# Adjacency build of a graph network kernel: narrow one-hots made four at a time on VectorE, a smaller share on GpSimd, and registers loaded in eights

## What is computed

```
x = layernorm(x + GCN(x))      # three rounds of  relu(layernorm(A_norm (h W) + b)),  A with self loops
x = layernorm(x + SUM(x))      # A (x W^T + b)
x = layernorm(x + GIN(x))      # two-layer MLP with batch norm of (1 + eps) x + A x
x = layernorm(x + RGCN(x))     # two rounds, per relation: mean over the edges of one type, summed
```

## Time and profile before

| | |
|---|---|
| median of 3 runs | 3174.41 us (3173.7 to 3174.66) |
| the profiled execution | 3173.94 us, span of its record 3172.1 us |
| build, from the first product to the last copy out of a bank | 67.3 to about 469.7 us |
| first and last transpose issued | 81.8 and 461.0 us (24 of them, 23 octaves between) |
| VectorE busy in those 379.2 us | 346.9 us |
| granted TensorE clock in them | 0.86 of full |

### The profile page before, as it was taken

The page is one execution under the profiler, slowest core; times in us unless marked ns, Lnnn a source line. Parts: engine busy times, 40 slices in busy tenths (PEclk is TensorE's granted clock), DMA queues, the critical chain, the costliest instruction groups (busy, mean ns, idle before and its releaser), DMA issues.

```text
span 3172.1 us, 51345 instructions
## 1 busy us (share of the span) xinstructions
PE 1767.6 (56%) x10220; PEld 947.7 (30%) x10220; DVE 1839.9 (58%) x6822; ACT 409.3 (13%) x868; POOL 1859.6 (59%) x2045
## 2 busy tenths in 40 slices
PE   4766669998954444444444446984444444444447
PEld 2222225444432222222222225762222222222227
DVE  6989986896334544444444445664444444444445
ACT  2444441111130000000000002530000000000003
POOL 2777760000027777777777773127777777777773
PEclk8888888999975555555555557995555555555558
DMA  2443440017022222222222221122222222222221
GB/s 62 102 104 96 93 114 7 1 38 222 1 60 57 53 54 53 54 53 54 53 54 53 53 54 44 79 76 53 54 53 54 53 54 53 54 53 54 53 54 30
DMA packets 174998, 191.76 MB, mean 60 GB/s; under 512 B 110508, under 2 KB 140989, under 8 KB 174722
## 3 DMA queue, kind: packets, MB, share of 16 engines
q0 software_dynamic: 50048, 102.60, 12.4%
q10 hardware_dynamic: 84924, 40.88, 5.5%
q1 hardware_dynamic: 39750, 45.01, 4.3%
HBM read 130.57 MB, written 38.14 MB: 53 GB/s over the span
## 4 chain that ended last, share of the span: by engine, by line
POOL 40%; PE 19%; issue 14%; DVE 13%; DMA 7%; SPq 4%; ACTq 2%; ACT 1%; DVEq 0%; POOLq 0%
POOL adj L775 40%; DMA adj<-table,adj 6%; DVE hi_hot L1240 6%; PE banks L552 5%; PE banks L537 4%; SPq L421 3%; PE banks L671 3%; DVE lo_hot L1248 2%; PE banks L683 2%; PE banks L723 1%; DMA adj_copy<-adj 1%; SPq L374 1%; DVE deg_in L1408 1%; PE banks L656 1%; PE banks L509 1%
## 5 line engine op out<-in xcount | busy, mean ns | idle before, releaser
L775 POOL DMA_INDIRECT adj<-table,adj x1564 | 1478.8, 946 | 511.2 <-issue 455.0
L627 PE MATMUL banks<-adj 128*128 x3908 | 807.0, 285 | 1174.3 <-DVE adj L1535 772.7
L1550 DVE TENSOR_TENSOR adj<-adj,banks 128x129 f32 x1954 | 566.0, 290 | 1000.0 <-PE banks L627 920.6
L627 PEld LDWEIGHTS banks<-adj 128*128 128x128 f16 x3908 | 406.5, 104 | 1579.9 <-issue 1534.3
L1535 DVE TENSOR_SCALAR adj<-adj 128x128 f16<-128x128 f16 x1954 | 550.8, 282 | 1.5
L755 POOL TENSOR_SCALAR lo_hot<-minus_iota,zT 128x128 f16<-128x128 f16 x392 | 312.3, 813 | 143.8 <-PE banks L509 92.0
L509 PE MATMUL banks<-hi_hot,lo_hot 128*128 128x400 f16 x977 | 273.8, 392 | 141.3 <-DVE hi_hot L1240 64.6
L1240 DVE TENSOR_SCALAR hi_hot<-iota,zT 128x400 f16<-128x400 f16 x977 | 271.5, 339 | 32.9 <-PE banks L509 32.2
L762 POOL MEMSET adj<- 128x32 f16 x1 | 0.1, 127 | 421.6 <-PE banks L552 421.6
L552 PE MATMUL banks<-adj,split 128*128 128x512 f16 (+1 forms) x1078 | 216.8, 359 | 0.0
L509 PEld LDWEIGHTS banks<-hi_hot,lo_hot 128*128 128x128 f16 x977 | 103.4, 106 | 312.0 <-issue 259.3
(11 more groups left out here) (242 smaller groups left out, 1280.1 us busy)
## 6 DMA issues: line engine op xcount, KB each, us to landing
adj<-table,adj POOLq DMA_INDIRECT x1564, 2.5
adj_copy<-adj ACTq DMA_DIRECT2D x25, 800.0 KB, 3.9
adj<-adj_copy SPq DMA_DIRECT2D x6, 2176.0 KB, 16.4
table<-adj SPq DMA_DIRECT2D x25, 512.0 KB, 2.6
adj<-adj_copy SPq DMA_DIRECT2D x1, 3072.0 KB, 10.4
adj<-adj_copy SPq DMA_DIRECT2D x3, 1024.0 KB, 15.7
table<-split SPq DMA_DIRECT2D x6, 256.0 KB, 2.3
out_dram<-xres SPq DMA_DIRECT2D x6, 256.0 KB
```

The costliest lines, as they stand in the source:

```text
L627: m = e.matmul(bank[j % NSUM][:, 0:b - a], hot[:, j % NHOT, :], edge[:, a:b], start=(q == 0), stop=(q == 1), skip_group_check=True)
L775: e.indirect_dma_start(gath[:, (t + 1) % NG, 0:2 * D], None, table, bass.IndirectOffsetOnAxis(ap=index[:, which, t:t + 1].bitcast(U32), ax ...
L1550: e.tensor_tensor(a, a, bank[j % NSUM][:, 0:D + 1], ALU.add).then_inc(accumulated, 1)
```

## The change

Four things are changed in the build.

1. VectorE makes the narrow one-hots of a group with one `tensor_tensor` of 128 x 4 elements instead of four `tensor_scalar` of 128. The slot then holds the four steps interleaved, column by column, so TensorE takes its stationary operand with a step of four elements for those groups (`by_column`). GpSimd's groups keep the old layout (`by_step`). The comparison is now with a positive row (`iota`, `iota4`), and the plan writes the edge's number twice, as fp32 (`nlo`) and as fp16 (`lo`).
2. GpSimd makes one group of three, 82 instead of 98 of the 245. VectorE makes 163.
3. There are ten slots for wide one-hots instead of eight, and they are made eight steps ahead instead of six.
4. SyncE and ScalarE load their registers eight at a time instead of 32: 31 loads instead of 8, and 25 instead of 7. TensorE's loads stay.

```
-POOL_SHARE = (2, 5)
+POOL_SHARE = (1, 3)
+GATES, ENDS = 8, 8
...
+        lo = zT[:, 3 * JA - JA // 2 - 1:3 * JA].bitcast(F16)
...
-        NLO, NHI, NWIN = 8, 8, 8
-        AHEAD_LO, AHEAD_HI = 5, 6
+        NLO, NHI, NWIN = 8, 10, 8
+        AHEAD_LO, AHEAD_HI = 5, 8
...
-        minus_iota = sb("minus_iota", [P, P], F16, own)
-        lo_hot = sb("lo_hot", [P, NLO, LG, P], F16, own)
+        iota4 = sb("iota4", [P, P, LG], F16, own)
+        lo_hot = sb("lo_hot", [P, NLO, P * LG], F16, own)
+        by_step = lo_hot.rearrange("p s (k n) -> p s k n", n=P)
+        by_column = lo_hot.rearrange("p s (n k) -> p s n k", k=LG)
...
             for g in range(NGATE):
-                if g % REGS == 0:
-                    n = min(REGS, NGATE - g)
+                if g % GATES == 0:
+                    n = min(GATES, NGATE - g)
                     e.load(gate_regs[0:n], gate_row[:, g:g + n])
...
-                e.matmul(banks[:, bass.ds(c, 1), 0:NC].rearrange("p o n -> p (o n)"), lo_hot[:, g % NLO, j % LG, :],
+                low = by_step[:, g % NLO, j % LG, :] if by_pool(g) else by_column[:, g % NLO, :, j % LG]
+                e.matmul(banks[:, bass.ds(c, 1), 0:NC].rearrange("p o n -> p (o n)"), low,
                          hi_hot[:, j % NHI, :], start=False, stop=True, skip_group_check=True).then_inc(crossed, 1)
...
-                    e.tensor_scalar(lo_hot[:, g % NLO, k, :], minus_iota[:, :], nlo[:, j:j + 1], None,
+                    e.tensor_scalar(by_step[:, g % NLO, k, :], iota[:, 0:P], nlo[:, j:j + 1], None,
                                     ALU.is_equal).then_inc(low_pool, 1)
...
             for w in range(NWA):
-                k = w % REGS
+                k = w % ENDS
                 if k == 0:
-                    n = min(REGS, NWA - w)
+                    n = min(ENDS, NWA - w)
                     e.load(end_regs[0:n], end_row[:, w:w + n])
...
-                e.tensor_scalar(nlo[:, a0:a0 + n], sets[0][:, 0:n], -1.0, None, ALU.mult).then_inc(own_dve, 1)
+                e.tensor_copy(lo[:, a0:a0 + n], sets[0][:, 0:n]).then_inc(own_dve, 1)
+                own.up()
+                e.tensor_copy(nlo[:, a0:a0 + n], sets[0][:, 0:n]).then_inc(own_dve, 1)
...
-                    for j in steps_of(g):
-                        e.tensor_scalar(lo_hot[:, g % NLO, j % LG, :], minus_iota[:, :], nlo[:, j:j + 1], None,
-                                        ALU.is_equal).then_inc(low_dve, 1)
+                    k, n = g * LG, len(steps_of(g))
+                    e.tensor_tensor(by_column[:, g % NLO, :, 0:n], iota4[:, :, 0:n],
+                                    lo[:, k:k + n].unsqueeze(1).broadcast_to([P, P, n]), ALU.is_equal).then_inc(low_dve, 1)
```

More of the change, by code:

```diff
@@ L145, in gnn_stack @@
         gate_row = zT[64:65, 2 * JA:2 * JA + NGATE].bitcast(I32)
-        assert 3 * JA + NWA <= NP and NWORD <= JA and NGATE <= JA
+        assert 3 * JA + NWA <= NP and NWORD <= JA // 3 and NGATE <= JA // 3
         tab_i = carve([P, 3, TB, P], I32)
@@ L294, in gnn_stack @@
         for g in range(NG_LO):
-            made[by_pool(g)] += len(steps_of(g))
+            made[by_pool(g)] += len(steps_of(g)) if by_pool(g) else 1
             low_at[g] = made[by_pool(g)]
@@ L367, in _ @@
             e.dma_start(scr_t, rows_i[:, 1, :]).then_inc(plan_out, 16)
-            gate_regs = [e.alloc_register(f"gate{i}") for i in range(REGS)]
+            gate_regs = [e.alloc_register(f"gate{i}") for i in range(GATES)]
             least = e.alloc_register("least_free")
@@ L371, in _ @@
             for g in range(NGATE):
-                if g % REGS == 0:
-                    n = min(REGS, NGATE - g)
+                if g % GATES == 0:
+                    n = min(GATES, NGATE - g)
                     e.load(gate_regs[0:n], gate_row[:, g:g + n])
-                e.reg_alu(least, gate_regs[g % REGS], 1, ALU.max)
+                e.reg_alu(least, gate_regs[g % GATES], 1, ALU.max)
                 e.wait_ge(window_free, least)
@@ L745, in _ @@
                    allow_small_or_imprecise_dtypes=True).then_inc(iotas_set, 1)
-            e.iota(minus_iota[:, :], pattern=[[-1, P]], base=0, channel_multiplier=0,
+            e.iota(iota4[:, :, :], pattern=[[1, P], [0, LG]], base=0, channel_multiplier=0,
                    allow_small_or_imprecise_dtypes=True).then_inc(iotas_set, 1)
@@ L850, in _ @@
             e.wait_ge(ends_row, 1)
-            end_regs = [e.alloc_register(f"window_end{i}") for i in range(REGS)]
+            end_regs = [e.alloc_register(f"window_end{i}") for i in range(ENDS)]
             least = e.alloc_register("least_crossed")
             for w in range(NWA):
-                k = w % REGS
+                k = w % ENDS
                 if k == 0:
-                    n = min(REGS, NWA - w)
+                    n = min(ENDS, NWA - w)
                     e.load(end_regs[0:n], end_row[:, w:w + n])
```

## The result

| | before | after |
|---|---|---|
| median | 3174.05 us (4 runs beside it) | 3149.18 us (3148.28 to 3149.99) |
| ratio | | 0.9922, interval 0.9905 to 0.9939 |
| span of the record | 3172.1 us | 3148.1 us |
| first product | 67.3 us | 68.1 us |
| first and last transpose | 81.8 and 461.0 us | 81.0 and 434.6 us |

The kernel became 24.9 us faster, 0.8%. Where the build ends, it leads by 26.4 us (434.6 against 461.0 for the last transpose): 25.6 of that come from the 23 octaves, 0.8 from a first transpose that is issued sooner.

A forecast was written before the change was run, and what follows sets the result against it. VectorE and ScalarE level bound the build, ScalarE late next: 23 octaves of 14.95 + 0.3 us save 28.4, the start 2.3, so 3173.94 becomes 3143.2, median 3144; forecast 3134 to 3152 (0.55), 8 in 10 3133 to 3167.

The forecast's parts named there:

- The bound now: Build before the change: VectorE (15.08 us an octave) and ScalarE (14.96) level, 16.49 paid as neither hides the other's hiccups.
- its total does not fall: ScalarE in the build: four loads of eight cost what one of 32 did, so it still needs 14.95 us an octave.
- The narrow one-hots: VectorE in the build: one instruction of 0.42 us, taken as 0.38 with overlap; VectorE falls to 13.0 us an octave.
- The weighing by the Trainium skill: VectorE's narrow one-hots: four small instructions come to 4 x 183 cycles, one large to 407, so the fixed part decides.
- ScalarE's register loads: ScalarE in the build: a load of eight registers in each octave, taken at 1.95 us.
- The idle that I left, 0.3 us an octave: ScalarE's octaves in the build: 0.3 us of idle left where 1.54 was, bounds 0 and 1.3.
- The start: Plan and first octave: plan +1.2 us, first product -1.1, first octave -1.2; together -2.3, first transpose near 79.5 us.
- The gate: Sign in the build: TensorE's wait for SyncE's gate, 44 us without the start, falls to some 15.
- Rival 1: VectorE in the build: the port shared with GpSimd makes VectorE late, 14.4 to 15.1 us an octave; 3158 us, chance 0.25.
- Rival 2: Register loads in the build: small loads do not do what they should; 3167 us, or 3172; chance 0.11.
- Rival 3: TensorE in the build: stationary loads with a step of four take 0.4 us instead of 0.1; 3195 to 3345 us, chance 0.06.

The follow-up runs named there:

- e2: The changed kernel with SyncE's and ScalarE's register loads both back to 32: ratio 0.9896 to the kernel before, 15.07 us an octave.
- e12: The kernel before with packed window ends, loaded by ScalarE midway in an octave, and SyncE's loads of eight; VectorE's work as before: ratio 0.9963, octave 15.75 us.
- e8: The changed kernel with VectorE's four narrow one-hots still one instruction but stored step by step: ratio 0.9938 to the kernel before, octave 15.50 us.
- e3: The changed kernel with ScalarE's loads back at 32 registers, SyncE's at eight: ratio 0.9878 to the kernel before, octave 14.86 us.
- e4: The changed kernel with SyncE's loads back at 32 registers, ScalarE's at eight: ratio 0.9916 to the kernel before, octave 15.37 us.
- e7: The changed kernel with ScalarE's load of eight moved from behind the transpose to the octave's fifth window: ratio 0.9857 to the kernel before, octave 14.42 us.
- e10: The changed kernel with two window ends packed into one word, ScalarE loading 32 words midway in an octave: 3120.88 us, ratio 0.9836 to the kernel before.
- e1: The kernel before with only SyncE's and ScalarE's register loads cut to eight: ratio 0.9967, octave 16.00 us.
- e6: The changed kernel with GpSimd making two groups of five again: ratio 0.9921 to the kernel before, octave 15.42 us.
- e9: The changed kernel with ScalarE loading 32 registers at the fifth window of every fourth octave, SyncE's at eight: ratio 0.9878 to the kernel before, octave 14.57 us.

## Why the prediction was right, and where it was off

**The bound now.** Right in the main. VectorE and ScalarE nearly level was the reading on which all hung, and e2 and e12 bear it out: cut one engine's work and the other holds. ScalarE's side was miscounted, though. I let six loads of 32 fall into the 23 octaves. Seven are issued in all, one ahead of the first transpose (61.5) and the last, of four registers, behind the last transpose (466.5 against 461.0), so five are left, and five octaves of 20.5 to 20.8 us show them. ScalarE needed 13.0 + 5 x 7.49 / 23 = 14.6 us an octave, not 14.96. The forecast does not use this number, but "its total does not fall" rests on it.

**The narrow one-hots.** 0.42 us forecast for the instruction, 0.412 measured, and of the bounds the fast one held (the engine advances by 0.33 us for each, where 0.38 was taken); e8 shows the slow one, 0.675 against the 0.66 taken from the fp32 rows. VectorE came to 13.46 an octave against 13.0. The excess lies in the wide ones, 270.82 us where 240 plus overlap was taken; their mean went from 339 to 347 ns. The weighing by the Trainium skill (VectorE: DVE Perf Modes, The perf-mode tier table) held too: four small ones cost 0.66 to 0.83 us (four times the prediction's 91 to 114 us over 549), one large one 0.33.

**ScalarE's register loads.** This is the term that was mis-sized. I took 1.95 us, from a load of TensorE's that stood alone, and bounded it by 2.18. Behind a transpose it is 2.40. The 7.49 of the earlier trace rows held the same half microsecond once, and I divided it by four. "Its total does not fall" was too mild: it rises, by 0.5 us an octave from the size of the load and by another 0.3 from the miscount above, 14.6 to 15.4. e3, e4 and e7 show the size from three sides. With 12.95 + 2.45, ScalarE's octave is 15.4, not 14.95.

**The idle that I left, 0.3 us an octave.** Nothing was left: 22 octaves within 0.2 us of each other. That term was my own choice, and its bound of 0 is what held. The two errors have opposite signs, so the octave came to 15.37 against 15.25, and the 23 of them to 353.6 us against 350.8. This closeness is luck: with the load at its true cost and the idle as I chose it, the sum would have been some 3154, past the 3152 at which the forecast ended. What I said of the bound was right, that ScalarE is late next; what I said of the time was right in part by two errors that cancel.

**The start.** The first transpose came at 81.0, not 79.5. The plan ended 2.7 us later, not 1.2. The two copies explain 1.15. The rest is in the input's landing and the products of the plan, ahead of any changed instruction. Over the ten other runs that have the new plan the first product stands between 67.0 and 69.3 us, so I take it for scatter, without having shown it. The end of the plan scatters too: SyncE's first copy of the plan to DRAM begins at 58.3 us before, at 61.0 after, and from 58.8 to 62.2 in those ten.

**After the build.** The lead of 26.4 us at the last transpose is 24.0 at the end of the record. The missing 2.4 arise in steps of under 1 us over the dense and the relation stages, where nothing was changed. What makes them stays open; single runs of one kernel differ by 1.7 us. The three gaps, 2.8 us in the octaves, 1.5 at the start and 2.4 behind the build, are the 6.7 between the 3143.2 forecast for the profiled execution and its 3149.93.

**The gate.** I expected TensorE's wait for SyncE to fall from 44 us to 15 as a sign. It is 56.3. The sign was badly chosen: SyncE only hands on ScalarE's cleared banks, so that wait now measures ScalarE as well as SyncE's loads. In e7 it is 36.6, in e10 26.6, in e1, where VectorE is the bound, 4.2.

**The rivals.** Rival 1 (the port between VectorE and GpSimd) did not come: the new instruction shows no blocking, its middle 80% lie between 405 and 419 ns. The wide ones are longer beside GpSimd, 359 against 317 ns, and e6 measures the exchange. Why they grew by 8 ns on average over the kernel before, at a lower share of GpSimd, is open: beside GpSimd they took 346 ns there. In this case's traces the rule of the Trainium skill (SBUF — State Buffer, Who interferes with whom) shows on the `tensor_scalar` side, not on the instruction with two inputs; and even there one wide one in ten lasts 421 ns or more, against at most 326 behind another with no GpSimd instruction beside it, so what is added is some 0.1 us and not the 0.6 us or more that an instruction of GpSimd lasts. Rival 2 (the loads bring nothing) was half right, for another reason: ScalarE's loads cost, SyncE's were idle. Rival 3 (the stationary operand) fell: a load with a step of four elements takes 113 ns instead of 96, and by the record TensorE never waited for one. So the step costs 18%: less than the factor of four that rival 3 priced, and more than the full rate that it quotes.

## What to carry to other kernels

Add up what an engine's sequencer does (register loads, issues of DMAs) before calling the engine idle: here ScalarE was busy for 47% of the stretch by the record (165.71 of 353.60 us) and had no time to spare. Where two engines are level, a gain on one is worth only what the other leaves, and a change with several parts should be timed part by part, each where its engine is the bound: here one half took back 0.3 us an octave of the other. Splitting a long stop into short ones brings a fixed cost with each short one (here four loads took 9.6 us for one of 7.45), which has to be less than what the long one left uncovered.

## What the runs showed of the hardware that was not expected

**A register load behind a transpose.** On ScalarE a load of eight takes 2.40 us right behind the issue of a transpose and 1.75 midway; of 32, 7.45 and 6.81. Loads of other engines that begin while a transpose is being issued last longer, and nearly all of them end only after it; one that begins shortly ahead of it can be stretched too. In the change SyncE's are 1.67 us in the middle, 2.94 where one begins 0.8 us ahead of a transpose (at 126.66) and 6.30 where one begins 0.3 us into it (at 297.48).

**Register loads come in two speeds.** These are all loads of the changed kernel outside ScalarE's (SyncE's gates and TensorE's words, eight registers each, in the build; then SyncE's 32, TensorE's eight and VectorE's 32 in the relation stage):

```profile
L378 SPq TENSOR_LOAD <-zT x31: 1663/1668/6300, 62.9 to 421.0; - x31
...
L504 PEldq TENSOR_LOAD <-zT x16: 768/1950/6412, 65.7 to 427.0; - x16
...
L425 SPq TENSOR_LOAD <-rows x48: 1860/1864/2075, 943.0 to 3035.3; - x48
...
L623 PEldq TENSOR_LOAD <-rows x246: 308/591/604, 901.8 to 3082.1; - x123
...
L1551 DVEq TENSOR_LOAD <-rows x62: 1353/2101/2833, 928.7 to 3067.5; - x62
```

SyncE takes 1.86 us for 32 registers in the relation stage, and 6.5 for 32 in the build. TensorE takes 0.59 and 1.95 for eight. On ScalarE it is 6.81 in e9 and 1.95 in e10, for 32 numbers from the same partition of the same tile at the same kind of place. What differs is where in `zT` they start. The slow ones begin at word 1954 + 8k or 1954 + 32k (gates, words) or 2931 + k (ends), none of them a multiple of four; e10's begin at 1956, 1988 and 2020, all multiples of four, and so do the fast tables in `rows`. e10's own first load points the same way: two registers from word 1954 of the very same table took 691 ns, in line with the slow pace (four took 1112 in e7) and not with 32 in 1946. A start at a multiple of 16 bytes, counted from the start of the tile, would explain all of them, at some 0.06 us a register instead of 0.2. That is a reading of runs made for other ends; no run changed the start alone. If it holds, moving three tables by one to three words would take most of the loads' time out of the build.
